# Expert weights kept on chip and addressed by a register on TensorE, with expert tiles of 256 rows

## The chip, the cores and the metric

The kernel runs on one core of one Trainium2 chip. The metric is the device time of one execution in microseconds (us). One core has five engines that run at the same time and meet through semaphores: TensorE (PE, matmuls; PEld is its loading of the stationary operand), VectorE (DVE), ScalarE (ACT), GpSimd (POOL) and SyncE (SP, which here only issues transfers). A "q" behind an engine's name (PEldq, SPq) marks its sequencer.

## The reference

64 images of 196 tokens pass through a patch projection to 192 features, an attention layer with 12 heads, and a layer of 8 experts of which each token uses 2. Only the last is touched by the change:

```python
h = relu(x @ Wr1.T + br1);  score = h @ Wr2.T + br2
_, idx = top_k(score, 2)
w = softmax(where(mask, score, -inf))
for e in range(8):
    mid = relu(x @ W1[e].T + b1[e])      # 192 -> 768
    ye = mid @ W2[e].T + b2[e]           # 768 -> 192
    out = out + w[..., e:e + 1] * ye
```

There are 12,544 tokens, so 25,088 pairs of a token and an expert.

## The kernel before, in words

The kernel has two phases. The attention phase computes everything up to the input of the experts; it writes the normed rows to `split_rows`, and packs the weights of each expert (split into high and low 16-bit parts, with the biases) into `packed` in memory, 3,168 columns of 2 bytes for each half expert and partition. The expert phase (`expert_phase`, line 1334) is what the change touches. In it the tokens come in 49 groups of 256 (`GT`).

Router, one group `g` at a time: SP loads the rows (`load_rows`), PE transposes them (`transpose_rows`), computes the hidden layer of the router and the scores (`router_hidden`, `router_scores`), DVE picks the two experts (`route`), PE and DVE count each token's place in its expert's list (`count`, `find_place`), and POOL sends the rows to `slots`, a list in memory for each expert, with four indirect DMAs (`send`, line 2082).

Experts, one tile `i` at a time: a tile is `T` = 512 successive rows of one expert's list. While groups still arrive, DVE chooses for each new tile the expert with the most waiting rows (`select`, line 1796: eleven small dependent operations); this gives the first `FULL` = 42 tiles. The last `REST` = 14 tiles are planned when all groups are in (`plan_rest`), may overlap rows that were done, and so have their destinations masked (`dest`, `keep`, `instead`). `NT` = 56 tiles in all.

For a tile, SP reads the expert's number and the first row from SBUF into registers (`value_load`, lines 1521 and 1522), loads that expert's packed weights into one of `DEEP` = 3 buffers `wst` (line 1525, 1,584 KB), loads the rows transposed into `xT` (line 1533), and then their token numbers and gates (`tail`). On PE a tile is `FCH` = 6 steps, one for each 128 of the 768 hidden features. `hidden(n)` makes the 128 x 512 block of step `n` in one PSUM bank with five matmuls (lines 1616 to 1622). ACT takes the block as bf16 (`mh`, line 2021), DVE the remainder (`ml`, line 1923). `project(n)` multiplies both into the tile's output, 12 matmuls of 192 columns (lines 1636 to 1639), `LAG` = 2 steps behind `hidden`. After the sixth step four bias matmuls follow (line 1643), ACT and DVE evict two 128-row blocks each, scaled by the gates, into one of two `y_out` buffers (`evict`), and POOL adds the four blocks to the rows of the result with four indirect DMAs (`add_rows`, line 2097). The adds of a tile wait until all adds of the tile before have landed.

The order on every engine is written out by hand. The phase begins with `COMPUTE` = 10 router groups by themselves (the prologue). Then come the mixed iterations: six expert steps each (one tile), and in them one router group at fixed steps, the transposes behind step 0, `count` at 1, `router_hidden` at 2, `router_scores` at 4. After group 48 the iterations have expert steps only. POOL's order in an iteration is `number_tokens`, `add_rows`, `send`. Tile 0 waits until group 7 (`SELECT` - 1) has been sent. PE's weight operands in `hidden` and `project` are slices of `wst[q]` with addresses that are fixed when the kernel is built.

Of the kernel before, what the change touches and what calls it, by code (L numbers as in the profile page):

```python
# [6 lines left out]
F16 = mybir.dt.float16  # L7
# [8 lines left out]
P = 128  # L16
IMAGES = 64
TOKENS = 196
DIM = 192
# [39 lines left out]
T = 512  # L59
TJ = T // P  # L60
NT = (2 * ROWS_ALL + EXPERTS * (T - 1)) // T
# [12 lines left out]
DEEP = 3  # L74
# [3 lines left out]
SELECT = EXPERTS  # L78
COMPUTE = SELECT + 2
REST = NT - FULL  # L80
# [1253 lines left out]
def expert_phase(nc, packed, slots, total_rows, split_rows, router):  # L1334

    ctx = ExitStack()
    with ctx:
# [88 lines left out]
        wst = [sb(f"wst{i}", [P, 2, PACK], BF16) for i in range(DEEP)]  # L1426
# [8 lines left out]
        mh = [sb(f"mh{i}", [P, T], BF16) for i in range(MID)]  # L1435
        ml = [sb(f"ml{i}", [P, T], BF16) for i in range(MID)]
        y_out = [sb(f"y_out{i}", [P, TJ, DIM]) for i in range(2)]

        mid_bank = [ps(f"mid_bank{i}", [P, 512]) for i in range(MID_PS)]
# [27 lines left out]
        w_in = [sem(f"w_in{i}") for i in range(DEEP)]  # L1467
# [25 lines left out]
        ITERATIONS = NT + COMPUTE  # L1493
# [7 lines left out]
        def tile_there(i):  # L1501
            return 0 <= i < NT

# [3 lines left out]
        def _(sp):  # L1507
# [7 lines left out]
            def load_tile(i):  # L1515
# [7 lines left out]
                wait(sp, used, FCH * (i - DEEP + 1))  # L1523
# [6 lines left out]
                last = i + SELECT - 1  # L1530
                if last < FGROUPS:
                    sp.wait_ge(sent[last % RING], SENT * (last // RING + 1))
# [8 lines left out]
            for it in range(ITERATIONS):  # L1541
                load_rows(it + AHEAD)
                if tile_there(it - SELECT):
                    load_tile(it - SELECT)
# [4 lines left out]
        def _(pe):  # L1549
# [53 lines left out]

            def hidden(n):
                i, c = n // FCH, n % FCH
                q = i % DEEP
                if c == 0:
                    pe.wait_ge(w_in[q], 16 * (i // DEEP + 1))
                    pe.wait_ge(xT_in[q], 16 * (i // DEEP + 1))
                wait(pe, ml_ready, n - MID_PS + 1)  # L1610
                o = mid_bank[n % MID_PS][:]

                def w(b, k=P):
                    at = b * PART + (c % PCHUNKS) * P
                    return wst[q][0:k, c // PCHUNKS, at:at + P].bitcast(F16)
                nc.tensor.matmul(o, w(0), xT[q][:, 0, :], start=True, stop=False)  # L1616
                nc.tensor.matmul(o, w(1), xT[q][:, 1, :], start=False, stop=False)  # L1617
                nc.tensor.matmul(o, w(2), xT[q][:, 2, :], start=False, stop=False)  # L1618
                nc.tensor.matmul(o, w(3), xT[q][:, 0, :], start=False, stop=False)  # L1619
                if c == 0:  # L1620
                    pe.wait_ge(xe_ready, i + 1)
                nc.tensor.matmul(o, w(4, HI + 3), xe[q][:], start=False, stop=True).then_inc(mid_ready, 1)  # L1622

            def project(n):
                i, c = n // FCH, n % FCH
                q = i % DEEP
                pe.wait_ge(ml_ready, n + 1)
                if c == 0:
                    wait(pe, evicted, TJ * i)
                at = W1_COLS + (c % PCHUNKS) * DIM  # L1630
                high = wst[q][:, c // PCHUNKS, at:at + DIM]
                low = wst[q][:, c // PCHUNKS, W2_COLS + at:W2_COLS + at + DIM]
                for j in range(TJ):
                    cols = slice(j * P, (j + 1) * P)
# [553 lines left out]
```

## Time and profile before

| what | us |
| --- | --- |
| runs, median (lowest to highest) of 3 | 2078.61 (2074.81 to 2085.45) |
| profiled execution: its span; the page gives no other time of it | 2041.0 |
| PE busy | 1849.8 (91%) |
| DVE busy | 1458.3 (71%) |
| ACT busy | 1287.1 (63%) |
| POOL busy | 1139.5 (56%) |

Busy time is the sum of an engine's instructions in the profiled execution; matmuls are pipelined, so a busy PE need not run at its peak, and the distance between starts says more. Times in rows count from the start of the span. In a timeline a row with "x10" holds ten instructions in a row, and the bracket at its end says how long the engine had been idle and what ended that. The expert phase begins at 1144.7 us.

### The profile page before, as it was taken

What the parts mean: (1) busy time and instruction counts of PE and PEld (TensorE: products, weight loads), DVE (VectorE), ACT (ScalarE), POOL (GpSimd) and SP (SyncE); (2) the same over time, 40 slices, a digit from 0 to 9 for tenths busy, and PEclk for the clock granted to TensorE, in tenths of its full rate; (3) what the DMA queues carried; (4) which work ended last, traced back from release to release, by engine and by line L of the source; (5) the groups of instructions that cost most, each with busy time, mean ns of one, the idle gap of its engine ahead of it and who ended that gap; (6) DMA issues with size and microseconds to landing.
All of it is one profiled execution on the core that took longest, in us unless ns stands there. A gap on an engine that the chain in (4) does not pass through costs nothing. (4 is left out here: it accounts for less than half of the span.)

```text
span 2041.0 us, 54475 instructions
## 1 busy us (share of the span) xinstructions
PE 1849.8 (91%) x18013; PEld 1378.2 (68%) x18013; DVE 1458.3 (71%) x4506; ACT 1287.1 (63%) x2661; POOL 1139.5 (56%) x1070
## 2 busy tenths in 40 slices
PE   4898998899889989898898579999999999999996
PEld 4666766666666666666665457777777777767774
DVE  4798889888988898889887456565665655574442
ACT  4688888888888888888888334444444444433332
POOL 4345464645555555555552356766767667664444
PEclk8898999999999999999998569999999999999998
DMA  4586665656566565656554358887888889878985
GB/s 154 147 253 195 186 203 166 196 181 192 174 191 189 179 185 180 194 185 192 174 173 120 102 175 194 197 211 192 199 216 195 198 206 197 198 188 182 187 183 83
DMA packets 362520, 373.10 MB, mean 183 GB/s; under 512 B 144516, under 2 KB 326080, under 8 KB 358272
## 3 DMA queue, kind: packets, MB, share of 16 engines
q1 hardware_dynamic: 320704, 329.03, 55.3%
q0 software_dynamic: 41664, 42.12, 12.3%
q8 instruction: 86, 1.41, 0.3%
q14 instruction: 66, 0.54, 0.1%
HBM read 223.20 MB, written 125.83 MB: 171 GB/s over the span
## 5 line engine op out<-in xcount | busy, mean ns | idle before, releaser
L2021 ACT ACTIVATE mh<-mid_bank 128x512 bf16<-128x512 f32 x336 | 200.6, 597 | 415.2 <-PE mid_bank L1622 415.2
L1923 DVE SCALAR_TENSOR_TENSOR ml<-mid_bank,mh 128x512 bf16<-128x512 f32 x336 | 232.0, 690 | 320.0 <-ACT mh L2021 319.3
L874 DVE TENSOR_REDUCE row_max<-s_bank 98x2 f32<-98x392 f32 x768 | 394.2, 554 | 53.6 <-PE s_bank L650 51.6
L1072 ACT ACTIVATE probs<-t_bank 98x392 f32<-98x392 f32 x768 | 339.7, 499 | 103.9 <-PE t_bank L666 100.5
L2097 POOL DMA_INDIRECT out_rows<-y_out,tail x168 | 267.4, 1592 | 160.7 <-DVE y_out L1957 114.1
L1636 PE MATMUL y_bank<-wst,mh 128*128 128x192 bf16 x1344 | 330.7, 246 | 0.8 <-DVE y_out L1957 0.8
L1639 PE MATMUL y_bank<-wst,ml 128*128 128x192 bf16 x1344 | 330.7, 246 | 0.0
L1638 PE MATMUL y_bank<-wst,mh 128*128 128x192 bf16 x1344 | 330.5, 246 | 0.0
L650 PE MATMUL s_bank<-k_stack,q_stack 96*98 96x196 f16 x1536 | 234.6, 259 | 46.2 <-DVE row_max L874 32.9
L1248 POOL TENSOR_TENSOR x_lo<-x_buf,x_hi 128x588 f16<-128x588 f32 x128 | 170.5, 1344 | 175.1 <-DVE x_b L939 73.0
L666 PE MATMUL t_bank<-q_stack,k_stack 104*98 104x196 f16 x1536 | 225.3, 259 | 32.8 <-ACT probs L1072 29.6
L2082 POOL DMA_INDIRECT slots<-row_r,spot x196 | 191.5, 977 | 81.9 <-issue 56.7
L650 PEld LDWEIGHTS s_bank<-k_stack,q_stack 96*98 96x98 f16 x1536 | 143.4, 126 | 99.6 <-DVE row_max L874 88.3
L666 PEld LDWEIGHTS t_bank<-q_stack,k_stack 104*98 104x98 f16 x1536 | 151.1, 128 | 74.7 <-ACT probs L1072 70.1
L558 PE MATMUL p_bank<-wtok_h,x_hi 128*98 128x192 f16 x768 | 192.0, 250 | 9.9 <-POOL x_lo L1248 9.7
L560 PE MATMUL p_bank<-wtok_h,x_lo 128*98 128x192 f16 x768 | 191.4, 249 | 0.0
L559 PE MATMUL p_bank<-wtok_l,x_hi 128*98 128x192 f16 x768 | 191.3, 249 | 0.0
L679 PE MATMUL o_bank<-probs,v_buf 98*32 98x196 f32 x3072 | 174.3, 346 | 4.0 <-ACT probs L1072 2.1
L1096 ACT COPY q_stack<-m_bank 8x784 f16<-8x784 f16 x192 | 154.4, 804 | 6.1 <-PE m_bank L690 1.5
L1636 PEld LDWEIGHTS y_bank<-wst,mh 128*128 128x128 bf16 x1344 | 134.2, 100 | 24.5 <-issue 4.7
L1638 PEld LDWEIGHTS y_bank<-wst,mh 128*128 128x128 bf16 x1344 | 130.9, 97 | 19.3
L2097 POOL DMA_INDIRECT out_rows<-y_out,dest x56 | 86.9, 1552 | 92.9 <-DVE gate L1945 36.8
(257 smaller groups left out, 4527.6 us busy)
## 6 DMA issues: line engine op xcount, KB each, us to landing
wst<-packed SPq DMA_DIRECT2D x56, 1584.0 KB, 8.3
x_buf<-in_x_t SPq DMA_DIRECT2D x32, 1176.0 KB, 7.9
q_stack<-stack_parts SPq DMA_DIRECT2D x288, 98.0 KB, 2.5
k_stack<-stack_parts SPq DMA_DIRECT2D x288, 98.0 KB, 2.6
stack_parts<-qk_hi SPq DMA_DIRECT2D x32, 588.0 KB, 2.9
stack_parts<-qk_lo SPq DMA_DIRECT2D x32, 588.0 KB, 3.1
out_rows<-h_buf SPq DMA_DIRECT2D x32, 294.0 KB
h_in<-out_rows SPq DMA_DIRECT2D x32, 294.0 KB
```

Of the source, the lines that this page charges most:

```text
L558: nc.tensor.matmul(out, x_hi[:, f, tokens], wtok_h[:, f, :], start=(f == 0), stop=False)
L650: last = nc.tensor.matmul(s_bank[hh % 2][0:HALF, u, 0:TOKENS], q_stack[st.q][0:PARTS, head, head_cols(st, u)], k_stack[st.q][0:PARTS, head ...
L666: last = nc.tensor.matmul(out, k_stack[st.q][:, head, head_cols(st, v)], q_stack[st.q][:, head, head_cols(st)], start=True, stop=True)
L874: nc.vector.reduce_max(row_max[st.odd][:, :, hh:hh + 1], s_bank[hh % 2][0:HALF, :, 0:TOKENS], AX.X).then_inc(max_ready, 1)
L1072: nc.scalar.activation(probs[st.odd][:, hh], t_bank[hh % 2][0:HALF, :, 0:TOKENS], ACT.Exp).then_inc(probs_ready, 1)
L1636: nc.tensor.matmul(o, mh[n % MID][:, cols], high, start=(c == 0 and j % 2 == 0), stop=False, skip_group_check=True)
L1638: nc.tensor.matmul(o, mh[n % MID][:, cols], low, start=False, stop=False, skip_group_check=True)
L1639: last = nc.tensor.matmul(o, ml[n % MID][:, cols], high, start=False, stop=False, skip_group_check=True)
L1923: nc.vector.scalar_tensor_tensor(ml[n % MID][:], mid_bank[n % MID_PS][:], 0.0, mh[n % MID][:], ALU.max, ALU.subtract).then_inc(ml_ready, 1)
L2021: nc.scalar.activation(mh[n % MID][:], mid_bank[n % MID_PS][:], ACT.Relu).then_inc(mh_ready, 1)
L2082: nc.gpsimd.indirect_dma_start(out=slots, out_offset=bass.IndirectOffsetOnAxis(ap=spot[g % RING][:, j, k:k + 1], axis=0), in_=row[g % RING ...
L2097: nc.gpsimd.indirect_dma_start(out=total_rows, out_offset=bass.IndirectOffsetOnAxis(ap=to, axis=0), in_=y_out[q][:, j, :], in_offset=None, ...
```

## The change

Tiles have 256 rows; `NT` becomes 105, `FULL` 91, `REST` 14. All weights are loaded once, in eight DMAs on ACT's queue at the start of the phase, into one SBUF tensor `weights`; the first `hidden` waits for all of them. PE reads the number of the tile's expert from SBUF into a register of its own (`find_expert`), and the weight operands of `hidden` and `project` and the bias operand are slices of `weights` at that register. SP no longer reads the expert's number nor loads weights. A step is still one 512-column PSUM bank: it holds two chunks (`CH` = 2) of 128 features for 256 rows, so a tile is `TSTEPS` = 3 steps, with ten hidden matmuls of 256 columns and twelve project matmuls of 192 columns each, then two bias matmuls. Both blocks of a tile are in the same `y_bank`, and one engine evicts them (ACT for even tiles, DVE for odd). `DEEP` becomes 6. `SELECT` becomes 4 and `COMPUTE` 6, so the prologue has six groups; the expert steps begin in the middle of iteration 6 and end in iteration 59 (`LAST`). DVE selects two tiles in an iteration, both at step 3. POOL's order in a mixed iteration is `add_rows` of one tile at step 1, `send` at step 2, `add_rows` of the next tile at step 4. Tile 0 waits until groups 0 to 3 have been sent.

```diff
-T = 512
+T = 256
+BANK = 512
+CH = BANK // T
+TSTEPS = FCH // CH
-DEEP = 3
+DEEP = 3 * CH
-SELECT = EXPERTS
+SELECT = (EXPERTS * (T - 1) + 2 * GT) // (2 * GT)
 COMPUTE = SELECT + 2
+OFFSET = FCH * COMPUTE + (FCH - TSTEPS)
...
-        wst = [sb(f"wst{i}", [P, 2, PACK], BF16) for i in range(DEEP)]
+        weights = sb("weights", [P, 2 * EXPERTS, PACK], BF16)
...
+        def groups_for(i):
+            return SELECT + -(-T * i // (2 * GT))
+        def y_bank_of(i, j):
+            return (i * TJ + j) // 2 % 2
...
             def load_tile(i):
...
-                e = sp.value_load(expert_i[0:1, i:i + 1], min_val=0, max_val=EXPERTS - 1)
                 at = sp.value_load(base_i[0:1, i:i + 1], min_val=0, max_val=EXPERTS * CAP - T)
...
-                sp.dma_start(wst[q][:], packed.rearrange("(e t) p n -> e t p n", t=2)[bass.ds(e, 1)]
-                             .rearrange("o t p n -> p (o t) n")).then_inc(w_in[q], 16)
                 if i == 0:
-                    for g in range(SELECT - 1):
+                    for g in range(SELECT):
                         sp.wait_ge(sent[g], SENT)
...
+            def find_expert(i):
+                if tile_there(i):
+                    if i < FULL:
+                        pe.wait_ge(selected, PICK * (i + 1))
+                    else:
+                        pe.wait_ge(plan, TILES_KNOWN)
+                    expert[i] = pe.value_load(expert_i[0:1, i:i + 1], min_val=0, max_val=EXPERTS - 1)
+            def part(i, t):
+                return weights[:].rearrange("p (e t) n -> p e t n", t=2)[:, bass.ds(expert[i], 1), t, :].rearrange(
+                    "p o n -> p (o n)")
...
             def hidden(n):
...
+                for k in range(CH):
+                    c = n % TSTEPS * CH + k
+                    o = mid_bank[n % MID_PS][:, k * T:(k + 1) * T]
+                    def w(b, rows=P):
+                        at = b * PART + (c % PCHUNKS) * P
+                        return part(i, c // PCHUNKS)[0:rows, at:at + P].bitcast(F16)
...
             def project(n):
...
+                if n % TSTEPS == 0:
+                    wait(pe, evicted, TJ * (i - CH + 1))
+                for k in range(CH):
+                    c = n % TSTEPS * CH + k
+                    at = W1_COLS + (c % PCHUNKS) * DIM
+                    high = part(i, c // PCHUNKS)[:, at:at + DIM]
+                    low = part(i, c // PCHUNKS)[:, W2_COLS + at:W2_COLS + at + DIM]
+                    for j in range(TJ):
...
-            for it in range(COMPUTE, ITERATIONS + 1):
+            find_expert(0)
+            for it in range(COMPUTE, LAST + 1):
                 for c in range(FCH):
-                    n = FCH * (it - COMPUTE) + c
+                    n = FCH * it + c - OFFSET
...
+                    if n >= 0 and (n + 1) % TSTEPS == 0:
+                        find_expert((n + 1) // TSTEPS)
...
+            for e in range(EXPERTS):
+                act.dma_start(weights[:, 2 * e:2 * e + 2, :], packed[2 * e:2 * e + 2].rearrange("t p n -> p t n")
+                              ).then_inc(w_in, 16)
             take_xt(0)
...
-                add_rows(it - COMPUTE - 1)
-                send(it - 1)
+                for c in range(FCH):
+                    n = FCH * it + c - OFFSET
+                    if n % TSTEPS == 1:
+                        add_rows(n // TSTEPS - 1)
+                    if c == 2:
+                        send(it - 1)
```

## Rows read from the trace of the kernel before

**Rows 1.** The page's busy tenths and PE clock in 40 slices.

```profile
PE   4898998899889989898898579999999999999996
PEclk8898999999999999999998569999999999999998
```

**Rows 2.** Windows: from:to, length, busy time of each engine, PE clock, DMA share, GB/s.

```profile
1220.00:1847.00 627.00, 624.74 (x5591) 474.01 (x5590) 384.72 (x1718) 262.61 (x529) 419.76 (x359) 1.00 0.83 199
1314.00:1318.00 4.00, 4.00 (x45) 3.23 (x43) 2.65 (x12) 2.12 (x5) 1.88 (x3) 1.00 0.98 395
```

**Rows 3.** Timeline of TensorE in one mixed iteration: start, length, engine, line, operation.

```profile
1226.85 0.38 PE L1616 MATMUL mid_bank<-xT,wst 128*128 128x512 f16 x1
...
1227.93 1.26 PE L1566 MATMUL r_bank<-xt,wr 128*128 128x256 f16 x10
1229.02 0.25 PE L1636 MATMUL y_bank<-wst,mh 128*128 128x192 bf16 x1
...
1230.01 0.38 PE L1616 MATMUL mid_bank<-xT,wst 128*128 128x512 f16 x1
...
1232.09 0.38 PE L1616 MATMUL mid_bank<-xT,wst 128*128 128x512 f16 x1
...
1243.06 1.26 PE L1566 MATMUL r_bank<-xt,wr 128*128 128x256 f16 x10
```

**Rows 4.** Timeline of TensorE in the prologue and at the first tile.

```profile
1164.03 0.17 PE L1589 MATMUL small_bank<-chosen,before 128*128 128x8 bf16 x1
1164.05 0.17 PE L1590 MATMUL small_bank<-chosen,ones 128*128 128x8 bf16 x1
...
1206.69 0.59 PE L1616 MATMUL mid_bank<-xT,wst 128*128 128x512 f16 x1 [9.96 <-DMA xT<-slots]
```

**Rows 5.** Timeline of GpSimd: the prologue, the last stretch, the end.

```profile
1177.21 0.96 POOL L2082 DMA_INDIRECT slots<-row_r,spot  x1 [0.30 <-issue]
...
1197.66 0.96 POOL L2082 DMA_INDIRECT slots<-row_r,spot  x1 [0.30 <-issue]
...
1913.51 1.55 POOL L2097 DMA_INDIRECT out_rows<-y_out,dest  x1 [6.90 <-DMA out_rows<-y_out,dest]
...
2027.33 1.55 POOL L2097 DMA_INDIRECT out_rows<-y_out,dest  x1 [2.73 <-DMA out_rows<-y_out,dest]
...
2032.90 1.55 POOL L2097 DMA_INDIRECT out_rows<-y_out,dest  x1 [0.30 <-issue]
```

**Rows 6.** The page's DMA issues: count, KB each, us to landing.

```profile
wst<-packed SPq DMA_DIRECT2D x56, 1584.0 KB, 8.3
```

**Rows 7.** Timeline of SP: the phase's first transfers and first transpose.

```profile
1144.71 40.53 SPq L1512 DMA_DIRECT2D row_r<-split_rows  x13
...
1201.58 1.62 SPq L1533 DMA_TRANSPOSE xT<-slots  x1
```

**Rows 8.** Timeline of VectorE: the last eviction.

```profile
2021.98 0.74 DVE L1957 TENSOR_SCALAR y_out<-y_bank,gate 128x192 f32<-128x192 f32 x2 [1.98 <-PE y_bank L1643]
```

**Rows 9.** Lines asked singly (two within 0.3 us): count, ns min/median/max, first and last start.

```profile
L645 PEldq EVENT_SEMAPHORE  x1: 51/51/51, 424.1 to 424.1; - x1
L91 PEldq FUSED_REGOPS  x1: 46/46/46, 424.2 to 424.2; - x1
L91 PEldq ALU_OP  x444: 32/32/36, 201.6 to 1001.6; - x148
L91 PEldq FUSED_REGOPS  x156: 42/46/60, 201.4 to 999.7; - x156
L1521 SPq TENSOR_LOAD <-expert_i x56: 271/283/487, 1191.6 to 1994.6; - x56
L1521 SPq FUSED_REGOPS  x56: 155/159/183, 1192.2 to 1994.9; - x56
```

**Rows 10.** Waits of GpSimd from 1300 to 1500: who for whom, us, times, longest.

```profile
POOL out_rows L2097 <- DVE y_out L1957: 34.1, 13, 2.7
```

More of the change, by code:

```diff
@@ L1465, in expert_phase @@
         plan = sem("plan")
-        w_in = [sem(f"w_in{i}") for i in range(DEEP)]
+        w_in = sem("w_in")
         xT_in = [sem(f"xT_in{i}") for i in range(DEEP)]
@@ L1540, in _ @@
                 load_rows(g)
-            for it in range(ITERATIONS):
+            loaded = 0
+            for it in range(LAST):
                 load_rows(it + AHEAD)
-                if tile_there(it - SELECT):
-                    load_tile(it - SELECT)
+                while loaded < FULL and groups_for(loaded) == it:
+                    load_tile(loaded)
+                    loaded += 1
+            for i in range(FULL, NT):
+                load_tile(i)
             sp.wait_ge(added, 16 * TJ * NT)
@@ L1602, in list_others @@
                     last.then_inc(spares_ready, 1)
+            expert = {}
+            def find_expert(i):
[8 more added lines that the diff above has]
+                    "p o n -> p (o n)")
@@ L1613, in w @@
[L1613 to L1619, printed above, removed]
@@ L1624, in project @@
+                last.then_inc(mid_ready, 1)
             def project(n):
-                i, c = n // FCH, n % FCH
-                q = i % DEEP
+                i = n // TSTEPS
                 pe.wait_ge(ml_ready, n + 1)
[L1628 to L1634, printed above, removed]
-                    o = y_bank[j // 2][:, j % 2, 0:DIM]
-                    nc.tensor.matmul(o, mh[n % MID][:, cols], high, start=(c == 0 and j % 2 == 0), stop=False,
-                                     skip_group_check=True)
-                    nc.tensor.matmul(o, mh[n % MID][:, cols], low, start=False, stop=False, skip_group_check=True)
-                    last = nc.tensor.matmul(o, ml[n % MID][:, cols], high, start=False, stop=False,
-                                            skip_group_check=True)
+                if n % TSTEPS == 0:
+                    wait(pe, evicted, TJ * (i - CH + 1))
@@ new lines, in project @@
+                for k in range(CH):
[4 more added lines that the diff above has]
+                    for j in range(TJ):
+                        cols = slice(k * T + j * P, k * T + (j + 1) * P)
+                        o = y_at(i, j)
+                        nc.tensor.matmul(o, mh[n % MID][:, cols], high, start=(c == 0 and j % 2 == 0), stop=False,
+                                         skip_group_check=True)
+                        nc.tensor.matmul(o, mh[n % MID][:, cols], low, start=False, stop=False, skip_group_check=True)
+                        last = nc.tensor.matmul(o, ml[n % MID][:, cols], high, start=False, stop=False,
+                                                skip_group_check=True)
@@ L1641, in project @@
                 if c == FCH - 1:
+                    biases = weights[:].rearrange("p (e t) n -> p e t n", t=2)[:, bass.ds(expert[i], 1), :,
+                                                                              PACK - BIAS_COLS:]
                     for j in range(TJ):
-                        last = nc.tensor.matmul(y_bank[j // 2][:, j % 2, 0:DIM], three[:],
-                                                wst[q][:, :, PACK - BIAS_COLS:], start=False, stop=True,
-                                                skip_group_check=True)
+                        last = nc.tensor.matmul(y_at(i, j), three[:], biases.rearrange("p o t n -> p (o t) n"),
+                                                start=False, stop=True, skip_group_check=True)
```

121 lines of the change are left out of this document (67 added, 54 removed).

## The prediction

> **What bounds the kernel now.** I read the page first (busy shares, the 40 slices), then windows over the second half, then the order of time on TensorE, GpSimd and the queues in one iteration. The page shows two halves; in the second, from slice 25 on, PE is 9 in nearly all slices at full clock [rows 1]. The diff touches only the expert half. There PE is busy 624.7 of 627 us between 1220 and 1847, DVE 385, ACT 263 and POOL 420 [rows 2]. Busy PE is not PE at its peak, so I check with spacing: a hidden step's five 512-column matmuls take from 1226.85 to 1227.93 (1.08 us, 216 ns each), a project step's twelve 192-column matmuls 1229.02 to 1230.01 (0.99 us, 82 ns each), and a whole step from 1230.01 to 1232.09 is 2.08 [rows 3]. That is one column per cycle at 2.4 GHz plus 2 to 3 ns, so the array has no gaps: only fewer columns, or idle time at the two ends, shortens this half. An iteration with a router group repeats every 15.13 us (the router's ten, 1227.93 to 1243.06) [rows 3].
>
> The half has two weak ends. Its start: ten groups go through the router alone, then PE idles for 9.96 us, to 1206.7, for the first tile's rows, and starts at half clock [rows 4, 1]. Its last stretch without router groups: the four scatter-adds of a tile of 512 leave 1.86 us apart and the next tile's begin 6.90 us after the last issue ends, 14.0 us for a tile, where six steps and four bias matmuls need 6 x 2.07 + 0.33 = 12.75 us; what ends that idle time is the landing of the adds before [rows 5].
>
> **The change, part by part.**
>
> *Fewer steps.* With 25,088 assigned rows, tiles of 512 need 56 slots (336 steps); tiles of 256 need 105 (315 steps of two 256-column chunks, the same 4,864 columns each). Hidden matmuls double in number; a 256-column one with its own weight load is priced by the router's ten, 1227.93 to 1229.02, 109 ns each [rows 3]: 10 x 109 = 1.09 us against 1.08, so a step is 2.08. The project matmuls are as before. Router groups in mixed iterations rise from 39 to 43, since the prologue falls from 10 groups to 6; one group costs the array 15.13 - 12.75 = 2.38 us. Array time before: 336 x 2.07 + 56 x 0.33 + 39 x 2.38 = 806.8. After: 315 x 2.08 + 105 x 0.17 + 43 x 2.38 = 775.4. Term: -31.4.
>
> *The start.* The weights of all experts (8 x 1,584 KB, 13.0 MB) now come in one go, issued on ACT's queue in front of its first copy, and the first hidden step waits for all of them. At the 395 GB/s of a window with a weight load in it they take 33 us from the phase's begin at 1144.7, so 1178; at the half's 199 GB/s 65 us, so 1210 [rows 2, 6]. The other condition is the rows of the first tile: it now waits for groups 0 to 3, whose last send ends at 1178.2 [rows 5]; for group 7 it was 3 us from the last send (ended 1198.6) to the transpose's issue at 1201.58 and 5 us more to the first matmul, so 1186 at the earliest [rows 4, 5, 7]. ACT may also be held in issuing eight large transfers, and sends and row loads share the DMA engines with the weights. I take 1198 against 1206.7: -9, between -20 and +30.
>
> *The stretch without router groups.* Weight loads (56 x 1,584 KB, the largest traffic) are gone, and so should be the late landings: where no load is in flight, an add lands and the next begins 2.7 us after the last issue ends (2.73 before 2027.33) [rows 5]. A tile's two adds then take 1.55 + 0.30 + 1.55 + 2.7 = 6.1 us against 6.41 of array time, so the wait is gone: -6 (1.3 in the tile shown, some 0.6 on the mean of ten). *The end:* from the last eviction's start (2021.98) to the end of the span are 19.0 us, in which the last two tiles' eight adds drain [rows 5, 8]. With two adds behind the last tile it is 0.74 + 0.7 + 3.4 + 6.55 (from the last issue's end at 2034.45 to 2041.0) = 11.4: -7.6.
>
> *Register addresses on TensorE.* This is what the array's sum does not show. The trace of before has no matmul addressed by a register. It has the parts: on PE's sequencer a register operation lasts 32 to 60 ns, but where two of its instructions follow each other they start at 424.1 and 424.2, so one takes about 0.10 us of the sequencer; in the attention loop there are 600 of them for 12 passes, about one for each different value [rows 9]. Loading the expert number costs SP 0.28 + 0.16 and gaps, some 0.6 us [rows 9]; I take 0.58. A pair of weight load and matmul takes the sequencer at most some 26 ns (right after a wait two follow at 1164.03 and 1164.05) [rows 4]. I count, per tile, 30 different weight addresses for hidden, 12 for project, one for the biases and one product: 44 x 0.10 = 4.4 us; 68 pairs x 0.026 = 1.77; the load 0.58; two waits of their own 0.2. Sum 6.95 us against 6.41 of the array: in the 20 tiles without router groups the sequencer is the bound, 20 x 0.54 = +11. In a mixed iteration the router adds 29 pairs and four waits, 1.15 us for two tiles, so 7.53 per tile against (6 x 2.08 + 0.34 + 2.38) / 2 = 7.60: level, with no slack. Waits of POOL are level there too: two adds (3.49), four sends of 0.97 + 0.30 behind 0.30 (5.1 without the last gap), 0.30, two adds (3.49), and 2.8 for landing and restart, 15.2 us [rows 5], against 15.20. Two engines level with the array lose by their ripple; DVE also gets a second select, eleven dependent operations, in one slot, which shortens the sequencer's lead. I put 0.25 us on each of 43 iterations: +11. Term: +22, between 0 (the operations slip in beside the 82 to 109 ns matmuls) and far more (below).
>
> Cost at nothing: evictions and the two conversions of a step keep 512 columns and their counts fall; the edge copy moves the same columns. If DVE's cover went, ml would come late; it is busy 61% [rows 2].
>
> Sum on the span: -31.4 - 9 - 6 - 7.6 + 22 = -32, so 2041.0 to 2009. The page gives the profiled execution only as its span; the median of the runs, 2078.6, lies 37.6 above it, and that part does not change. Forecast: **2047 us**; its own range, with the start at 1187 to 1225 and the sequencer term at 0 to 45, is 2022 to 2072.
>
> **Rivals.**
>
> *The sequencer costs nothing* (chance 0.13): address operations overlap decoding. For it: durations of 32 ns; against: starts 0.10 us apart. Time 2047 - 22 = 2025.
>
> *TensorE's sequencer becomes the bound outright: slower* (0.30). If each operand needs an operation of its own (30 hidden, 36 project, 2 bias), or a matmul with a register is handled more slowly than the plain pair, the sequencer needs 68 x 0.10 + 1.77 + 0.58 + 0.2 = 9.35 us in a tile without router and 9.9 in a mixed one: 20 x 2.9 + 85 x 2.3 = +256 for the +22, so 2281. It decides above 6.41 and 7.60 us: for the whole to be slower than before by 0.5% it needs +64 in place of +22, about 0.4 us per tile more. Half the 256 gives 2153. For it: the array has no slack and the count stands at the edge; against: waits with equal values share one operation in the attention loop. The Trainium skill (TensorE: Matmul & The Clock Gate, Back-to-back issue gap) has a rule that speaks for it: a matmul that the hardware does not decode costs the sequencer about 62 ns. In this trace plain pairs follow at 26 ns, so that path is not in use; if an address in a register led to it, 68 x (62 - 26) = 2.4 us per tile would be added, by estimate the same 2280.
>
> *The adds bound the mixed iterations* (0.12). The second tile's adds leave right behind the sends, and the two transposes of the next tiles are released then. Each us by which the landing is later than in the quiet case goes into all 43 iterations. At the 6.90 us wait of the loaded stretch it is +4 x 43 = 170; with no weight loads left I take +1: +43 on top, 2090, between 2060 and 2200. Against: before, adds beside a transpose in mixed iterations caused POOL no visible wait for landings [rows 10].
>
> **How the numbers follow.** Forecast 0.45, free sequencer 0.13, adds 0.12, sequencer bound 0.30. A change within 0.5% (10 us) can't be told from none. Faster by more: 0.45 + 0.13 and a quarter of the adds case, 0.61; within: 0.07; slower: 0.32. Below 2018 lies almost nothing; above 2215 the upper part of the sequencer case, some 0.15. The range is 2018 to 2215.
>
> **What would show it.** Right: 315 of each conversion, first hidden step near 1198, mixed iterations 15.2 to 15.6 us apart, tiles without router near 7.0, PE's idle time put down to issue or to its own sequencer, no load of weights in the loop, span near 2009. The free case shows 6.4; the slower one tiles of 8 us and more with matmuls 120 ns apart or wider. The adds case shows POOL waiting for landings in each mixed iteration and PE waiting for y_out or ml. A first hidden step after 1230 would break the start's term.

## The result: 2118 us, slower by 1.8%

| kernel | median of the runs | lowest to highest | profiled span | granted clock |
|---|---|---|---|---|
| before | 2082.03 (4 runs) | 2074.81 to 2086.73 | 2041.0; 2082.6 when profiled again | 0.955; 0.945 |
| changed | 2117.74 (4 runs) | 2116.37 to 2121.91 | 2114.6 | 0.942 |

The ratio is 1.0181, 95% interval 1.0159 to 1.0203. The forecast was 2047, faster than before. The measured time lies inside the stated range of 2018 to 2215, but the kernel became slower.

The page of the changed kernel, for [rows 1]:

```profile
span 2114.6 us, 62607 instructions
...
PE   4988998989998898999984599989999999999997
...
PEclk8999999999999999999986599999999999999998
...
q8 instruction: 115, 1.88, 0.4%
```

Windows of it (us of window, then busy per engine, clock, DMA share, GB/s), for [rows 2]:

```profile
1220.00:1847.00 627.00, 577.72 (x5941) 523.87 (x5939) 394.44 (x1992) 235.86 (x506) 366.98 (x319) 0.98 0.49 82
```

PE was busy 624.7 of 627 us and is now 577.7. The weight loads are gone from the loop as intended (199 GB/s became 82). TensorE has fewer columns to work, but it now stands idle for 49 of these 627 us. Its timeline at one place of the loop (idle time in brackets), for [rows 3]:

```profile
1414.29 0.39 PE L1574 MATMUL x_bank<-ident,row_r 128*128 128x128 f16 x4
1415.17 0.22 PE L1574 MATMUL x_bank<-ident,row_r 128*128 128x128 f16 x1 [0.50 <-issue]
1415.88 0.22 PE L1574 MATMUL x_bank<-ident,row_r 128*128 128x128 f16 x1 [0.49 <-issue]
1415.93 0.25 PE L1674 MATMUL y_bank<-weights,mh 128*128 x1
1417.31 0.24 PE L1676 MATMUL y_bank<-weights,mh 128*128 x1 [1.12 <-issue]
...
1418.13 0.24 PE L1676 MATMUL y_bank<-weights,mh 128*128 x1 [0.41 <-issue]
...
1418.92 0.29 PE L1676 MATMUL y_bank<-weights,mh 128*128 x1 [0.38 <-issue]
1419.01 0.36 PE L1677 MATMUL y_bank<-weights,ml 128*128 x1
1419.17 0.36 PE L1674 MATMUL y_bank<-weights,mh 128*128 x1
1419.33 0.36 PE L1676 MATMUL y_bank<-weights,mh 128*128 x1
```

In the middle of a run of matmuls that wait for nothing in the profile, single ones start 0.6 to 1.4 us apart. I call such a cluster of pauses a burst. After it 192-column matmuls start 0.16 us apart in place of 0.08: the granted clock is at the lower of its two levels from 1419.0 to 1422.4, after a stretch in which TensorE was busy 2.1 of 5 us. Two windows (columns as above):

```profile
1414.00:1419.00 5.00, 2.09 (x19) 1.17 (x17) 1.00 (x5) 0.89 (x2) 4.31 (x4) 1.00 0.49 97
1419.60:1420.50 0.90, 0.90 (x6) 0.62 (x5) 0.87 (x5) 0.90 (x3) 0.00 (x0) 0.50 0.71 88
```

Now GpSimd in the same stretch, for [rows 5, 10]:

```profile
1398.64 1.62 POOL L2148 DMA_INDIRECT out_rows<-y_out,tail  x1 [2.08 <-DVE y_out L2001]
1400.56 1.59 POOL L2148 DMA_INDIRECT out_rows<-y_out,tail  x1 [0.30 <-issue]
...
1406.40 1.56 POOL L2148 DMA_INDIRECT out_rows<-y_out,tail  x1 [4.10 <-DMA out_rows<-y_out,tail]
1408.27 1.57 POOL L2148 DMA_INDIRECT out_rows<-y_out,tail  x1 [0.30 <-issue]
1410.15 1.00 POOL L2133 DMA_INDIRECT slots<-row_r,spot  x1 [0.31 <-issue]
1411.45 0.98 POOL L2133 DMA_INDIRECT slots<-row_r,spot  x1 [0.30 <-issue]
1412.73 0.96 POOL L2133 DMA_INDIRECT slots<-row_r,spot  x1 [0.31 <-issue]
1414.00 0.96 POOL L2133 DMA_INDIRECT slots<-row_r,spot  x1 [0.30 <-issue]
1415.27 1.62 POOL L2148 DMA_INDIRECT out_rows<-y_out,tail  x1 [0.30 <-issue]
1417.19 1.57 POOL L2148 DMA_INDIRECT out_rows<-y_out,tail  x1 [0.30 <-issue]
```

Two adds, a wait for their landing (which [rows 10] did not have), two adds, four sends, and without a pause the next two adds: from 1406.40 on, 12.4 us in a row. The burst ends as the last add's issue does (1418.76). A run of that length is not new: before, four adds and four sends took 12.4 us in a row too. New is that adds stand directly behind the four sends. They do so in 13 of 41 iterations of the changed kernel, and in these TensorE loses 3.1 to 4.4 us in pauses (47 us in all); in the other 28 it loses 0.6 to 1.7 us (28 us in all). ScalarE's wait in the same stretch:

```profile
1409.33 0.60 ACT L2066 ACTIVATE mh<-mid_bank 128x512 bf16<-128x512 f32 x1 [1.49 <-PE mid_bank L1658]
1417.34 0.60 ACT L2066 ACTIVATE mh<-mid_bank 128x512 bf16<-128x512 f32 x1 [7.41 <-remote]
```

The first conversion starts 0.31 us after its step's last matmul (1409.02), which is the usual distance. The next step's last matmul started at 1412.09, and its conversion at 1417.34: TensorE's completion was seen five us late.

The stages, read from the timelines ("interval": from the router's ten matmuls to the next group's; "gaps": of matmul starts over 0.25 us apart, what lies beyond 0.1 us, summed from the first hidden step on; all columns in us):

| kernel | expert half begins | to first hidden step | from there to last matmul | interval, mean | gaps | to the end |
|---|---|---|---|---|---|---|
| before, first profile | 1144.7 | 62.0 | 815.0 | 15.13 | 7 | 19.3 |
| before, again | 1159.0 | 75.3 | 831.6 | 15.57 | 24 | 16.7 |
| changed | 1156.4 | 61.6 | 881.9 | 17.48 | 83 | 14.8 |

### The profile page after: what moved, and what is told of

The parts are those of the page before. It is cut to its first block and busy times, and to the rows that moved or that the text cites. A ratio compares the mean times of both kernels' runs of the same rounds, so it can differ in the third digit from the quotient of the medians.

```text
span 2114.6 us, 62607 instructions
## 1 busy us (share of the span) xinstructions
PE 1849.3 (87%) x19185; PEld 1508.9 (71%) x19185; DVE 1519.1 (72%) x5111; ACT 1274.2 (60%) x2683; POOL 1117.2 (53%) x1056
## 3 DMA queue, kind: packets, MB, share of 16 engines
q0 software_dynamic: 39648, 40.74, 12.4%
## 5 line engine op out<-in xcount | busy, mean ns | idle before, releaser
L2066 ACT ACTIVATE mh<-mid_bank 128x512 bf16<-128x512 f32 x315 | 188.0, 597 | 487.7 <-PE mid_bank L1658 296.9
L2148 POOL DMA_INDIRECT out_rows<-y_out,tail x182 | 287.7, 1581 | 280.1 <-DMA out_rows<-y_out,tail 109.3
L1965 DVE SCALAR_TENSOR_TENSOR ml<-mid_bank,mh 128x512 bf16<-128x512 f32 x315 | 216.9, 690 | 227.8 <-ACT mh L2066 215.1
L1677 PE MATMUL y_bank<-weights,ml 128*128 x1260 | 313.5, 249 | 9.9 <-issue 9.9
L1674 PE MATMUL y_bank<-weights,mh 128*128 x1260 | 313.2, 249 | 9.9 <-issue 8.9
L1676 PE MATMUL y_bank<-weights,mh 128*128 x1260 | 313.6, 249 | 7.5 <-issue 7.4
L1658 PE MATMUL mid_bank<-xe,weights 67*128 67x256 f16 x630 | 175.4, 278 | 6.5 <-issue 6.2
L1652 PE MATMUL mid_bank<-xT,weights 128*128 128x256 f16 x630 | 174.8, 277 | 5.8 <-issue 5.8
L1654 PE MATMUL mid_bank<-xT,weights 128*128 128x256 f16 x630 | 174.3, 277 | 4.2 <-issue 4.0
L1655 PE MATMUL mid_bank<-xT,weights 128*128 128x256 f16 x630 | 174.6, 277 | 2.2 <-issue 2.2
```

What stands on the lines that cost most here:

```text
L1658: last = nc.tensor.matmul(o, w(4, HI + 3), xe[q][:], start=False, stop=True)
L1674: nc.tensor.matmul(o, mh[n % MID][:, cols], high, start=(c == 0 and j % 2 == 0), stop=False, skip_group_check=True)
L1676: nc.tensor.matmul(o, mh[n % MID][:, cols], low, start=False, stop=False, skip_group_check=True)
L1677: last = nc.tensor.matmul(o, ml[n % MID][:, cols], high, start=False, stop=False, skip_group_check=True)
L1965: nc.vector.scalar_tensor_tensor(ml[n % MID][:], mid_bank[n % MID_PS][:], 0.0, mh[n % MID][:], ALU.max, ALU.subtract).then_inc(ml_ready, 1)
L2148: nc.gpsimd.indirect_dma_start(out=total_rows, out_offset=bass.IndirectOffsetOnAxis(ap=to, axis=0), in_=y_out[q][:, j, :], in_offset=None, ...
```

## Experiments

Line numbers of the experiments' kernels shift by a few. Four explanations are tested: "R", the register operations' own time on TensorE; "S", TensorE's supply of instructions, so that their number counts; "M", matmuls being slower when a register addresses them; "A", GpSimd's adds. By GpSimd's "ring" I mean its work for two tiles and one group, each part waiting for the one before: two adds, their landing, two adds, four sends, and the next adds.

**1. The kernel before, once more.** No edit.

> The kernel before, profiled once more. The profiled execution that the forecast was made from had a span of 2041.0 us, while its timed runs were 2075 to 2087; the changed kernel's span (2114.6) lies only 1.8 us below its own time (2116.37). If span and time always lie 2 us apart, the 37.6 us that the forecast carried along as a fixed part was a quick execution, and this profile has a span near 2075 to 2080, with the difference either in the attention half (the expert half began at 1144.7 then, 1156.4 in the changed kernel) or as idle time of TensorE in the expert half. If it is a fixed part outside of the span, the span is 2041 again.

Span 2082.6, time 2084.4. The profile that the forecast started from was a quick execution: 14.3 us in the attention half, 13.3 before the first hidden step and 16.6 behind it make up the difference, less 2.6 at the end. The 16.6 lie in the iterations: from the fifth on each is some 0.5 us longer, with one short pause of TensorE 1 to 3 us behind the last of the four sends. So span and time lie 2 us apart, and the 37.6 us that the forecast carried along as a part that does not change did not exist.

**2. A constant for the expert's number.**

```diff
-                    expert[i] = pe.value_load(expert_i[0:1, i:i + 1], min_val=0, max_val=EXPERTS - 1)
+                    expert[i] = i * EXPERTS // NT
```

> Changed kernel, but TensorE's number of the expert is a constant written at each tile (tile number x 8 / 105), so nothing is loaded into a register and no address is worked out (44 register operations, one load and one assertion per tile gone); some tiles take another expert's weights. Theory S (TensorE runs out of instructions: the changed kernel has 186 records per tile against 142, and in the iterations with a router group its weight loads stand still for 0.7 to 1.4 us each, in bursts of one to six, nearly 100 us in all): the stalls go, iterations 15.5 us apart, 2117.7 becomes 2040 to 2065. Theory R (the register operations' own time on TensorE's sequencer): the same gain, no stall, 2040 to 2065. Theory A (scatter-adds and their landings bound the iterations): no change, 2105 to 2118.

2093.8 us (ratio to before 1.0064, 1.0045 to 1.0083). None of the three expectations held: 24 us came back, but the mean interval is still 17.18 and the gaps sum to 66 us. The bursts now come every second iteration, of about 3 us each, and again where adds directly follow the four sends (18 iterations, 50 us; the other 23 have 12 us). GpSimd's waits in this kernel, over one such pair:

```profile
1412.67 1.62 POOL L2144 DMA_INDIRECT out_rows<-y_out,tail  x1 [0.30 <-issue]
...
1431.91 1.61 POOL L2144 DMA_INDIRECT out_rows<-y_out,tail  x1 [1.99 <-DVE y_out L1997]
...
1438.54 1.57 POOL L2144 DMA_INDIRECT out_rows<-y_out,tail  x1 [2.97 <-DMA out_rows<-y_out,tail]
...
1447.41 1.61 POOL L2144 DMA_INDIRECT out_rows<-y_out,tail  x1 [0.30 <-issue]
```

From the adds at 1431.91 over the landing to the next at 1447.41, which again had no pause before them, are 15.50 us: GpSimd's ring. TensorE needs 15.24 (below). Of the 61.7 us of gaps between 1230 and 1935, some 55.6 lie inside the issue of adds, which cover 308 us (the 0.30 us pause behind each issue counted to it); inside the issue of sends (210 us) lies at most 1 us. That is so in this kernel and not in all. In the changed kernel 41 of 75 us lie under adds and 8 under sends.

**3. One load of the number, registers kept.**

```diff
+                if i == 0:
+                    pe.wait_ge(selected, PICK)
+                    expert[0] = pe.value_load(expert_i[0:1, 0:1], min_val=0, max_val=EXPERTS - 1)
+                elif tile_there(i):
+                    expert[i] = expert[0]
```

> Changed kernel, but the number of the expert is loaded once, for the first tile, and used for all tiles; every weight operand is still addressed by a register, the 44 addresses are worked out once only and stay in registers. All tiles take the first tile's expert. Theory S (supply of instructions) and theory R (time of the register operations): like the kernel with constants, within 5 us, 2040 to 2065. A third one, M (a matmul whose address is in a register is itself handled more slowly, whoever wrote the register): the stalls stay and the time is 2105 to 2120.

2092.3 us, 1.0068 (1.0049 to 1.0087), like the constant. A matmul whose weights are addressed by a register is no slower; what costs is working the addresses out. Theory M is refuted.

**4. Resident weights with tiles of 512.**

```diff
-T = 256
+T = 512
-SHIFT = 8
+SHIFT = 9
```

> Changed kernel with tiles of 512 rows again (56 tiles, 336 steps of one chunk), weights of all experts resident and addressed by a register as in the changed kernel. Register operations per us of array time are halved (44 for a tile of 12.7 us), records of TensorE per us fall from 26 to about 20. Theory S: no bursts of stalls, mixed iterations near 15.15 us as before; 2065 to 2085, level with the kernel before. Theory R (44 x 0.10 us against 12.7): free too. Theory M: every hidden and project matmul is slowed, 2150 or more. It also shows what resident weights alone bring: if the adds land sooner without weight loads in flight, the stretch without router groups shortens from 14.0 us per tile to 12.75, some 10 us in all.

2090.6 us, 1.0048 (1.0030 to 1.0066): a little slower than before, and above the 2065 to 2085 that I expected. There are no bursts of 3 us, but pauses of 0.3 to 0.7 us in nearly every iteration; interval 15.65, 237.9 us from the last router group to the last matmul against 234.7 in the second profile of before. Taking the weight traffic away gained nothing.

**5. Constants, and waits in place of register operations.**

```diff
             def part(i, t):
+                for _ in range(2):
+                    pe.wait_ge(consts_set, CONSTS)
```

> The kernel with a constant for the expert's number (2093.8 us) plus two more waits on a long satisfied semaphore in front of each operand that the changed kernel addressed by a register: about 44 more instructions of TensorE per tile, none of them a register operation. Theory S (TensorE runs out of instructions; what costs is their number, in bursts of stalls): as the changed kernel or worse, 2110 to 2130, with stalls more often than every second iteration. Theory R (the register operations themselves cost, by their time): within 5 us of 2094.

2113.5 us, 1.0188 (1.0135 to 1.0242; two runs), the time of the changed kernel within its spread, with a mean interval of 17.56. The trace has 44 more waits per tile than that of experiment 2, and they cost 20 us. In the iterations with a router group, then, 44 waits do the same damage as 44 register operations, which supports S. Without router groups they do not: the tiles are 6.44 us apart in the median with the waits and without them, and 6.64 in the changed kernel. There the register operations and the load cost some 0.2 us per tile by themselves.

**6. No adds.**

```diff
-                        nc.gpsimd.indirect_dma_start(
-                            out=total_rows, ...
+                        nc.gpsimd.memset(idle[:, TJ * i + j:TJ * i + j + 1], 0.0).then_inc(added, 1)
```

> Changed kernel without its scatter-adds: each is replaced by a one-column memset of GpSimd that counts the same semaphore; the experts' share of the output is left out. Register operations and instructions of TensorE are those of the changed kernel. Theory A' (the bursts come where GpSimd, with four sends and four adds per iteration that wait for each other's landing, falls behind TensorE: in the kernel with constants the bursts lie beside two adds that directly follow the sends, every second iteration): bursts gone, mixed iterations 15.5 to 16.1 us instead of 17.5, span 2114 becomes 2040 to 2065. Theory S: bursts unchanged, 2100 to 2118.

2030.3 us (0.9787, 0.9746 to 0.9828; two runs), below the expected band, interval 15.42 in the median, 15.74 in the mean. All register operations are still there. The bursts of 3 us hang on the adds. Short pauses are left, and they follow the sends. GpSimd's last two sends of a group, ScalarE's next conversion and TensorE's next pause:

```profile
1438.68 0.96 POOL L2134 DMA_INDIRECT slots<-row_r,spot  x1 [0.31 <-issue]
1439.95 0.96 POOL L2134 DMA_INDIRECT slots<-row_r,spot  x1 [0.30 <-issue]
...
1441.85 1.08 ACT L2067 ACTIVATE mh<-mid_bank 128x512 bf16<-128x512 f32 x2 [4.35 <-remote]
...
1442.64 0.25 PE L1675 MATMUL y_bank<-weights,mh 128*128 x1 [0.36 <-issue]
```

In all 41 iterations a completion of TensorE that fell into the four sends was seen only 0.8 to 1.0 us after the last send's issue had ended, and all 19 us of pauses in them lie within 2 us behind it.

**7. Four output buffers.**

```diff
-        y_out = [sb(f"y_out{i}", [P, TJ, DIM]) for i in range(2)]
+        y_out = [sb(f"y_out{i}", [P, TJ, DIM]) for i in range(4)]
```

with the evictions' waits moved to the tile four before.

> Changed kernel with four buffers for the gated output of a tile instead of two, so that an eviction waits for the adds of the tile four before, no longer two before. Theory A'' (the link that closes the ring is eviction waiting for landed adds: ACT and DVE y_out late, POOL waits for them 134 us): mixed iterations fall below 16.5, 2117.7 becomes 2070 to 2095. Theory A' with GpSimd's own order as the link, or theory S: no change, within 5 us.

2110.8 us, 1.0186 (1.0147 to 1.0225), interval 17.32: the same ratio as the changed kernel's, and 7 us less at most by the medians. The evictions are not the link that closes the ring.

**8. The sends split.** Two at the old place, two behind the next tile's adds.

```diff
                     if c == 2:
-                        send(it - 1)
+                        send(it - 1, [0])
+                    if c == 4:
+                        send(it - 1, [1])
```

> Changed kernel with a group's four sends split on GpSimd: two at the place where all four stood, two behind the next tile's adds. No instruction is added or left out. If the run of four sends followed by two adds is what makes GpSimd late (A'), adds come earlier: bursts of 3 to 4.5 us disappear, mean mixed iteration below 16.8, 2117.7 becomes 2080 to 2105. If the bursts are TensorE's own (S), no change; if the later last send delays the tiles' transposes, slower, up to 2140.

2165.7 us, 1.0436 (1.0403 to 1.0469): slower. Two waits, us in total, times and longest, between 1300 and 1900, show why:

```profile
POOL out_rows L2148 <- DVE gate_m L1976: 189.7, 32, 8.5
...
ACT xe L2061 <- DMA xT<-slots: 151.9, 31, 7.9
```

The last sends of a group come later, so do the tile's transposed rows, and ScalarE waits for them in front of everything else in its order. The sum of TensorE's gaps rose to 102 us, 82 of them in front of `router_scores`, mostly under waits for ScalarE that the profile names: the split came with a shortage of lead.

**9. One add of a tile's two.**

```diff
+                        if j == 1:
+                            nc.gpsimd.memset(idle[:, i:i + 1], 0.0).then_inc(skipped, 1)
+                        else:
                             nc.gpsimd.indirect_dma_start(
```

> Changed kernel with the second of each tile's two scatter-adds left out (a one-column memset in its place; half of the experts' share of the output is missing). GpSimd is busy 3.4 us less per iteration, the wait for the landing of the tile before stays. If the bursts come from GpSimd's load (A': adds, landing, adds, four sends make a ring of 15.5 us where the array needs 15.4), they vanish wholly: mixed iterations 15.4 to 15.7, 2025 to 2045. If every add that is issued disturbs TensorE by itself, half of the loss stays: 2065 to 2080.

2047.0 us, 0.9835 (0.9801 to 0.9868; two runs), interval 16.28. Leaving half of the adds out brings 3.5% against the changed kernel's ratio, leaving out all of them 3.9%. The time is just above the band of the first expectation, but the trace fits neither of the two. The bursts of 3 us are gone with GpSimd's ring far from full, yet every iteration keeps about 1 us of pauses (46 us in all). None of them lies under an add: in the iterations with a router group all lie within 2 us behind the last of the four sends, as in experiment 6. So the four sends in a row do some of the damage without any full ring.

**10. One group of lead more, sends as they were.**

```diff
-COMPUTE = SELECT + 2
+COMPUTE = SELECT + 3
-DEEP = 3 * CH
+DEEP = 8
```

> Changed kernel whose experts start one router group later (one more group goes through the router alone, 42 mixed iterations instead of 43) and with eight tile buffers in place of six; sends and adds in the old order. The ring of GpSimd is the same, so A' expects the bursts to stay: mixed iterations near 17.3, start 5 to 7 us later: 2110 to 2125. A rival (late transposes, as ACT's copy of the edge waits for them, are what breaks the rhythm) expects mixed iterations below 16.3 and 2065 to 2085.

Here and in experiments 11 to 13 the edit also adds one wait of VectorE for its own gate steps. 2115.8 us, 1.0163 (1.0131 to 1.0196), interval 17.56, bursts as before: lead alone does nothing.

**11. Both: lead and split sends** (edits 8 and 10).

> The kernel before this one and the split of the sends in one: a group's four sends in two pairs, one behind each tile's adds, so that each landing is covered by sends and GpSimd's ring falls from 15.5 us to about 13; the router runs one group further ahead, so that the later sends do not delay the transposes, which is what made the split alone slower (2165.7; ACT waited 152 us for transposed rows). A': no bursts, mixed iterations 15.4 to 15.8, start 5 to 7 us later, 2035 to 2065, faster than the kernel before (2074 to 2082). If bursts come from sends beside the router's work and not from the ring, 2100 or more.

2050.9 us (0.9843, 0.9805 to 0.9882), interval 15.96, and one wait of GpSimd for a landing (1.8 us) in place of 27. A reordering without any work removed takes most of the loss back. It does not show that the full ring alone was the cause, since the split does two things: it puts two sends under each landing, and it ends the run of four sends. Two adds still follow two sends without a pause in 34 iterations, and only 6 of the 25 us of gaps between first and last router group lie there. A version that keeps the four sends together and only shortens the ring by reordering was not built.

**12. The same with a constant** (edits 8, 10 and 2).

> The faster order (router one group further ahead, eight tile buffers, sends split), with a constant for the expert's number on TensorE: no load, no register operation; some tiles take another expert's weights. In the changed kernel the same edit was worth 24 us, but there GpSimd's ring stretched the iterations. If the 44 register operations and the load cost only through the bursts, this is within 5 us of 2050.9 (7 us at most, from the tiles without router groups: 152.7 against 145.1 us for that stretch). If they cost by themselves, in every tile: 2025 to 2035.

2011.9 us (0.9689, 0.9666 to 0.9712), interval 15.24 with a smallest of 15.23: this is the array's own time, gaps 1.2 us in all. GpSimd still issues two adds directly behind two sends in 35 iterations, and TensorE does not pause once between the first and the last router group. The register operations and the load cost 32 us (by the ratios) to 39 (by the medians) here: by the two profiles 0.72 us in each of 40 intervals and 7.5 us behind the last router group. That is more than either expectation gave.

**13. Lead, split sends and four output buffers** (edits 8, 10 and 7): the best version.

> The faster order with four output buffers instead of two. The adds now stand in front of the sends at both tiles, so an eviction could be what waits for landed adds. If it is: mixed iterations from 15.96 to 15.5, 2030 to 2040. If not, within 4 us of 2050.9.

2031.3 us (2026.7 to 2035.0), ratio 0.9767, 0.9741 to 0.9793: faster than both kernels, inside the expected 2030 to 2040. Its waits of GpSimd from 1300 to 1840 (us in total, times, longest), and GpSimd's timeline over one interval:

```profile
POOL out_rows L2150 <- DVE gate_m L1978: 105.9, 33, 3.9
...
POOL out_rows L2150 <- DMA out_rows<-y_out,tail: 2.8, 2, 1.9
```

```profile
1431.60 1.61 POOL L2150 DMA_INDIRECT out_rows<-y_out,tail  x1 [3.46 <-DVE gate_m L1978]
1433.51 1.57 POOL L2150 DMA_INDIRECT out_rows<-y_out,tail  x1 [0.30 <-issue]
1435.38 1.00 POOL L2135 DMA_INDIRECT slots<-row_r,spot  x1 [0.30 <-issue]
1436.68 0.97 POOL L2135 DMA_INDIRECT slots<-row_r,spot  x1 [0.30 <-issue]
...
1437.99 1.61 POOL L2150 DMA_INDIRECT out_rows<-y_out,tail  x1 [0.18 <-issue]
1439.91 1.58 POOL L2150 DMA_INDIRECT out_rows<-y_out,tail  x1 [0.30 <-issue]
1441.80 1.00 POOL L2135 DMA_INDIRECT slots<-row_r,spot  x1 [0.30 <-issue]
1443.10 0.97 POOL L2135 DMA_INDIRECT slots<-row_r,spot  x1 [0.30 <-issue]
1446.70 1.61 POOL L2150 DMA_INDIRECT out_rows<-y_out,tail  x1 [2.63 <-DVE gate_m L1978]
```

The landing that took 4.10 us of idle time now passes under two sends, and GpSimd pauses 2.6 and 3.5 us in the two iterations shown. In the ring the third and fourth buffer were worth at most 7 us, here 16 (ratios) to 20.

| kernel | time | interval | gaps | last router group to last matmul |
|---|---|---|---|---|
| changed | 2117.7 | 17.48 | 83 | 152.7 |
| constant (2) | 2093.8 | 17.18 | 66 | 145.1 |
| no adds (6) | 2030.3 | 15.74 | 22 | 145.8 |
| lead and split (11) | 2050.9 | 15.96 | 33 | 162.8 |
| and constant (12) | 2011.9 | 15.24 | 1 | 155.3 |
| and four buffers (13) | 2031.3 | 15.66 | 20 | 159.9 |

(The last column of 11 to 13 is longer by some 10 us because the router is one group further ahead.)

## Why the prediction was wrong

The forecast for the span was 2009; it is 2114.6. The 106 us: attention half +12, start +9, from the first hidden step to the last matmul +82, end +3. The baseline error of about 36 us goes the other way, so that 2047 stands against 2118. Against the second profile of before (2082.6), which is closer to the usual run, the change gained 2.6 in the attention half, 13.7 at the start and 1.9 at the end, and lost 50.3 in between. That 2118 lies inside the stated range is no merit of the sum: its own range ended at 2072, and what lies above was there for the slower rivals.

*Fewer steps.* Right. With the constant and the split sends (12) the interval is 15.24, and the array's sum for it was 15.20; from the first hidden step to the last matmul it takes 777.5 us, where the forecast's array time was 775.4 with one router group more. The saving is there as soon as the pauses are gone.

*The start.* Half right. The first hidden step comes 61.6 us after the half begins. Against the profile that I used (62.0) nothing is gained in place of -9, and against the second (75.3) 13.7. The late begin (1156.4) belongs to the attention half, which varies by more than 14 us between executions of the same code.

*The end.* 14.8 us against 19.3 and 16.7: -4.5 or -1.9, not -7.6.

*The stretch without router groups.* GpSimd still waits for landings in four tiles (15.3 us), but TensorE stands idle for only 2 us between 1975 and 2100, so the landing is hidden from it, as forecast. Tiles are 6.66 us apart, and 6.43 with the constant:

```profile
2035.63 0.33 PE L1683 MATMUL y_bank<-weights,three 128*128 x2
...
2042.29 0.33 PE L1683 MATMUL y_bank<-weights,three 128*128 x2
```

```profile
2013.33 0.33 PE L1679 MATMUL y_bank<-weights,three 128*128 128x192 bf16 x2
...
2019.76 0.33 PE L1679 MATMUL y_bank<-weights,three 128*128 128x192 bf16 x2
```

*The register operations.* The count was right: each of the hidden step's lines has one per chunk and tile (105 x 6), which makes 44 per tile over all lines.

```profile
L1652 PEldq FUSED_REGOPS  x630: 46/46/46, 1216.1 to 2094.7; - x158
```

The size was near by luck: 22 forecast, 24 measured in the changed order (2 against changed), 32 to 39 in the order with split sends (12 against 11). The parts were not near. In a tile without router they cost 0.2 us, where 0.54 was forecast; the 0.10 us per operation had been read from two starts that are given to one decimal. In an iteration with a router group they cost 0.72 us in the better order (12 against 11), where the forecast had 0.25 for everything. Waits in their place cost as much there (5), so it is not a property of register operations; whether it is the number of instructions or the sequencer's time for them is not told apart, as a wait lasts 51 ns on it and a register operation 46. The Trainium skill (TensorE: Matmul & The Clock Gate, Back-to-back issue gap) gives 62 ns for a matmul that the hardware does not decode, which by the prediction's estimate would have been 2.4 us more per tile. No run here shows that: tiles with register addresses are 0.2 us longer, and with the addresses kept (3) the time is that of constants.

*The step that failed* is the one on GpSimd: "Waits of POOL are level there too", 15.2 us against 15.20, and with it "I put 0.25 us on each of 43 iterations". The interval became 17.48 us, so the loss is 2.3 us against the array's 15.20 and not 0.25; over 41 intervals it is some 80 us beyond the forecast, which is the whole of the +82. Two things were wrong in it. The ring is 15.50 us where the array needs 15.24 (from the end of the last add's issue to the next tile's add it takes 3.13 us, not 2.8; the other parts agree). And being level was priced by the overhang alone. A full ring pushes adds directly behind the four sends, and where that happens TensorE, which waits for none of them, pauses for 3 to 4 us (47 of 75 us of gaps). Nine times it then gets the lower clock level for 3.4 us or more, 34 us in all between the first and the last mixed group; in experiments 6 and 9, which have only the short pauses, that never happens. The other iterations lose 1 us each, and experiments 6 and 9 show that such short pauses follow four sends in a row even with the ring far from full.

The rival that names the adds as the bound (chance 0.12, 2090, 2060 to 2200) named the right engine and gave the nearest time. Its signs came in part: POOL waits for a landing in 23 of 34 iterations between 1300 and 1900 (77 us), not in each, and PE waits for y_out or ml for 0.8 us in all, behind the last router group; its pauses are put down to "issue", which the prediction had listed as a sign of being right. The rival's price was looked for in later landings; the price lay in TensorE's pauses beside GpSimd's sends and adds.

*The base.* One profiled execution, 38 us quicker than the median, was taken as the shape of all with a constant added. It showed intervals of 15.13 without any gap; the second shows 15.57. Of the 36 other executions of that kernel on record none was below 2067 us. A profile that lies so far below the runs' median is itself a sign that the slack read from it is not the usual one.

## What to carry to other kernels

When a change doubles the handshakes of a helper engine (here a wait for landed adds per 256 rows in place of per 512), add up that engine's ring, issue gaps and landing latency included, and compare it with the bottleneck's period. Here a ring that came out level cost 2 us of 15 per iteration, and it paid to break up the run of sends and put half of it under the latency. Interleaving independent transfers under a landing needs lead elsewhere: split or lead alone gave 2166 and 2116, both together 2051. Before a profile is used as the base, compare its span with the runs' median.

## What the runs showed of the hardware

- TensorE pauses for 0.3 to 1.4 us at a time, most often for about 0.7, in the midst of matmuls that wait for nothing in the profile, beside and right behind a run of GpSimd's indirect DMAs. Where two adds directly follow four sends it loses 3.1 to 4.4 us in the changed kernel (13 iterations) and 2.4 to 3.1 in experiment 2 (18). Behind four sends without adds it loses about 0.5 us (6) to 1 us (9). Behind two sends followed by two adds it loses nothing in experiment 12. The loss is larger when its own stream has more instructions (5).
- Its completions are seen late in the same stretches: behind four sends 0.8 to 1.1 us after the end of the last send's issue (41 of 41 iterations in 6 and in 9, all 35 late ones in 4). Counted by ScalarE's conversions that start over 0.3 us later than the usual 0.31 and for which it stood idle: 2 of 336 steps in the first profile of before, 41 in the second, 59 of 315 in the changed kernel, 44 (about 2.8 us each) even without adds, 11 in experiment 12. The first profile of before had the four sends in a row too, and no pause; why is open. By what path GpSimd's DMA issues, TensorE's instructions and its semaphore updates get in each other's way was not tried and stays open.
- Transfers of the page's "instruction" queue q8 grow with TensorE's instructions: 86 packets of 16 KB in the kernel before, 96 with the constant, 113 with the constant and the waits (5), 115 in the changed kernel. Between two of them lie some 255 records of TensorE in the median. The bursts keep no fixed place between two such packets.
- Register-addressed operands cost nothing if the addresses are kept: with 44 register operations in all (3) the time was that of constants (2092.3 against 2093.8), with 44 per tile it was 2117.7.
- The same program ran its attention half in 1144.7 and in 1159.0 us.
